# Edge pass of a graph network: gathered rows in four slots by parity of turns, attributes in another region

## The reference, cut to what matters

```python
src = edge_index[0]; dst = edge_index[1]          # 200000 edges, dst sorted
msg = jax.nn.relu(h[src] + edge_attr)             # h: [12500, 128], edge_attr: [200000, 128]
aggr = jax.ops.segment_sum(msg, dst, num_segments=n)
z = (1.0 + eps) * h + aggr                        # then two matmuls with batch norms
```

## Time and profile before

| | us |
|---|---|
| median of 3 runs | 16836.19 (16834.64 to 16855.76) |
| the profiled execution | 16957.4 |
| its span | 16955.6 |
| edge pass, first attribute load to PE's last halves (11797 to 14310) | 2513 |
| POOL busy in the whole span | 9653.8 (57%) |
| PE busy in the whole span | 6756.4 (40%) |
| DVE busy in the whole span | 3233.9 (19%) |

### The profile page before, as it was taken

The page is one execution under the profiler, slowest core; times in us unless marked ns, Lnnn a source line. Parts: engine busy times, 40 slices in busy tenths (PEclk is TensorE's granted clock), DMA queues, the critical chain, the costliest instruction groups (busy, mean ns, idle before and its releaser), DMA issues. The chain is left out here.

```text
span 16955.6 us, 119259 instructions
## 1 busy us (share of the span) xinstructions
PE 6756.4 (40%) x30243; PEld 5863.6 (35%) x30244; DVE 3233.9 (19%) x6147; ACT 824.7 (5%) x1247; POOL 9653.8 (57%) x9860
## 2 busy tenths in 40 slices
PE   3444443333334444410000009995555555533333
PEld 2333333333333333300000008873555554333333
DVE  3222221000011212200000014444111112311111
ACT  1000000000000000000000000003000000200000
POOL 2666666666666666667777440002666664366666
PEclk8555555555555555555555555557555555655555
DMA  2111111111111221233333212222222222221212
GB/s 87 47 48 47 48 48 45 48 48 48 48 47 53 55 55 54 57 87 100 100 100 99 66 33 87 97 89 84 82 81 80 82 82 89 67 54 52 54 53 53
DMA packets 593155, 1124.64 MB, mean 66 GB/s; under 512 B 220825, under 2 KB 364384, under 8 KB 566578
## 3 DMA queue, kind: packets, MB, share of 16 engines
q0 software_dynamic: 307488, 624.42, 14.6%
q1 hardware_dynamic: 285622, 499.73, 8.8%
HBM read 904.32 MB, written 218.95 MB: 66 GB/s over the span
## 5 line engine op out<-in xcount | busy, mean ns | idle before, releaser
L680 POOL DMA_INDIRECT work<-rows_a,index x4704 | 4587.5, 975 | 2399.1 <-issue 1544.6
L751 PE MATMUL psum<-onehot,work 128*128 128x64 f32 x12544 | 2822.4, 419 | 4459.8 <-DMA work<-rows_a,index 2818.1
L751 PEld LDWEIGHTS psum<-onehot,work 128*128 128x128 f32 x12544 | 2717.3, 328 | 4556.2 <-issue 4424.5
L680 POOL DMA_INDIRECT work<-rows_b,index x3136 | 3118.6, 994 | 1771.6 <-issue 1075.8
L1191 POOL DMA_INDIRECT work<-attention_rows,index x1568 | 1610.9, 1027 | 612.5 <-issue 557.2
L751 PE MATMUL psum<-onehot,regionB 128*128 128x64 f32 x6272 | 1551.9, 416 | 720.1 <-issue 581.2
L751 PEld LDWEIGHTS psum<-onehot,regionB 128*128 128x128 f32 x6272 | 1440.3, 327 | 819.6 <-issue 801.5
L846 DVE TENSOR_TENSOR regionA<-regionA,psum 128x64 f32 x2352 | 508.0, 216 | 5289.9 <-remote 2271.8
L765 PE MATMUL psum<-onehot,regionB 128*4 128x64 f32 (+1 forms) x6272 | 1174.7, 358 | 484.9 <-issue 484.5
L765 PEld LDWEIGHTS psum<-onehot,regionB 128*4 128x4 f32 (+1 forms) x6272 | 1023.8, 223 | 533.3 <-issue 486.8
L182 POOL COPY work<-regionB 128x500 f32 (+1 forms) x75 | 45.5, 606 | 2034.9 <-DVE regionB L561 2034.9
(11 more groups left out here) (253 smaller groups left out, 4471.5 us busy)
## 6 DMA issues: line engine op xcount, KB each, us to landing
gathered_rows<-work SPq DMA_DIRECT2D x98, 1088.0 KB
work<-gathered_rows SPq DMA_DIRECT2D x98, 1088.0 KB, 4.9
regionB<-in_edge_attr SPq DMA_DIRECT2D x195, 512.0 KB
work<-rows_a,index POOLq DMA_INDIRECT x4704
work<-rows_b,index POOLq DMA_INDIRECT x3136
work<-attention_rows,index POOLq DMA_INDIRECT x1568
x_transposed<-regionA SPq DMA_DIRECT2D x75, 250.0 KB, 6.0
rows_a<-regionC SPq DMA_DIRECT2D x50, 250.0 KB
```

The lines of the kernel that those rows point to most:

```text
L680: pool.indirect_dma_start(rows3[h][:, t, :], None, table, bass.IndirectOffsetOnAxis(ap=net.index[:, k, h * ST + t:h * ST + t + 1], axis=0) ...
L751: last = nc.tensor.matmul(bank_of(h, q, 0), msgs3[h][:, t, 0:D], onehot[:, h * ST + t, :], start=(k == 0), stop=(k == GT - 1))
```

## The change: what it does

In the edge pass the gathered rows get four buffers of 16 batches in region B: a pair (h = 0 and 1) for even turns and a pair for odd turns. The attributes move to `work`, and the messages lie in region B behind the four row buffers. Each row buffer has its own semaphore for landed gathers. POOL may fill a buffer when the messages that last used it are made, which is two turns earlier, not one: the counter `message[h]` starts at 2 and not at 1, and POOL's and ACT's conditions follow. At the start of a round POOL waits until all messages of the round before are made. DVE's loop over turns now runs 24 times over two turns, so that each addition knows its buffer at build time. The other passes keep their code.

```diff
-    rows3 = [r.rearrange("p (t f) -> p t f", f=width) for r in rows]
-    attr = [net.B[:, h * HALF * D:(h + 1) * HALF * D] for h in range(2)]
+    if edges:
+        rows = [[net.B[:, (k * 2 + h) * HALF * D:(k * 2 + h + 1) * HALF * D] for h in range(2)] for k in range(2)]
+    else:
+        rows3 = [r.rearrange("p (t f) -> p t f", f=width) for r in rows]
+    attr = [net.work[:, h * HALF * D:(h + 1) * HALF * D] for h in range(2)]
...
-    at0 = EPP * H if attention else 2 * HALF * D
+    at0 = EPP * H if attention else 4 * HALF * D
...
-    gathered = name("gathered") if attention else [net.pool_sem() for _ in range(S)]
+    gathered = name("gathered") if attention else [net.pool_sem() for _ in range(4 if edges else S)]
+    fills = [NIT - NIT // 2, NIT // 2]
...
-                                act.wait_ge(message[h], n + 2)
+                                act.wait_ge(message[h], n + 3)
...
+                    if edges:
+                        for h in range(2):
+                            pool.wait_ge(message[h], r * NIT + 2)
+                        pool.sem_inc(moved, 1)
...
+                            to = rows[k][h].rearrange("p (t f) -> p t f", f=D) if edges else rows3[h]
+                            landed = gathered[k * 2 + h] if edges else gathered[h]
                             for t in range(ST):
                                 pool.indirect_dma_start(
-                                    rows3[h][:, t, :], None, table,
+                                    to[:, t, :], None, table,
                                     bass.IndirectOffsetOnAxis(ap=net.index[:, k, h * ST + t:h * ST + t + 1], axis=0)
-                                ).then_inc(gathered[h], 16)
+                                ).then_inc(landed, 16)
...
-                    dve.sem_inc(message[h], 1)
+                    dve.sem_inc(message[h], 2 if edges else 1)
...
-                nc.vector.memset(net.B[:, 0:2 * HALF * D], 0.0)
+                nc.vector.memset(net.work[:, 0:2 * HALF * D], 0.0)
...
-                        dve.wait_ge(gathered[h], n * 16 * ST + 16 * ST)
+                        dve.wait_ge(gathered[k * 2 + h], (r * fills[k] + fill) * 16 * ST + 16 * ST)
                         dve.wait_ge(attr_loaded[h], n * 32 + 32)
-                        nc.vector.tensor_tensor(msgs[h], rows[h], attr[h], ALU.add).then_inc(message[h], 1)
+                        nc.vector.tensor_tensor(msgs[h], rows[k][h], attr[h], ALU.add).then_inc(message[h], 1)
...
+                if edges:
+                    with dve.Fori(0, NIT // 2) as j:
+                        for k in range(2):
+                            i = dve.snap(j * 2 + k)
+                            stage_index(net, dve.snap(i + 2), k).then_inc(index_ready, 1)
+                            for h in range(2):
+                                add(i, h)
+                                compare(dve.snap(i + 1), h)
+                                messages(dve.snap(i + 1), h, 1 - k, dve.snap(j + k))
```

More of the change, by code:

```diff
@@ L814, in compare, with messages @@
                             AX_X, ALU.add).then_inc(piled[h], 1)
-                def messages(i, h):
+                def messages(i, h, k=0, fill=0):
                     n = r * NIT + i
@@ L858, in _ @@
                     messages(0, h)
[L859 to L869, removed]
+                if edges:
[7 more added lines that the diff above has]
+                                messages(dve.snap(i + 1), h, 1 - k, dve.snap(j + k))
+                else:
+                    with dve.Fori(0, NIT - 1) as i:
+                        if not attention:
+                            following = dve.snap(i + ahead)
+                            stage_index(net, following, following % 2).then_inc(index_ready, 1)
+                        for h in range(S):
+                            add(i, h)
+                            if follow and h == S - 1:
+                                due_chunks(net, dve, i, i + 1, lambda c: follow.vector(dve, c),
+                                           lambda: all_added((r * NIT + i) * 2 * GPH + 2 * GPH))
+                            compare(dve.snap(i + 1), h)
+                            messages(dve.snap(i + 1), h)
                 for h in range(S):
```

## The result

The kernel after takes **16953.8 us** (16940.79 to 17003.71, 5 runs), the kernel before, timed again beside it, 16839.87 us (16834.64 to 16855.76, 5 runs). The ratio is 1.0084, with a 95% interval from 1.007 to 1.0097: 114 us slower. The forecast was 16860 us, no change. The time lies in the range of 16600 to 17000 us, but it is 94 us above the point, and slower was only the second likeliest direction.

What follows compares the result with a forecast made beforehand. PE, slowed beside running gathers, was taken to bound the edge pass. Terms 0 + 46 - 28 gave +18 us, +36 with the profiler's waits; +24 was taken: 16860 us, no change, range 16600 to 17000.

Steps and rivals of the forecast that it cites:

- What bounds the pass: Edge pass: PE bounds it, though not at its speed, losing 1065.7 us to "issue" and lacking work for 19.6 us.
- The signs named ahead: Edge pass near 2500 us, about 25 POOL waits of some 20 us, "issue" not smaller, slow stretches ending near pauses.
- Term (1): POOL's larger lead in the edge pass: more rows in store do not speed PE, 0 us; upper bound 433.5 us gained.
- Term (2): POOL released for whole turns: about 24.5 pauses of 20.3 us, 64 us more, 46 without the profiler; bounds -119 to +352.
- Term (3): End of the edge pass: POOL finishes further ahead, PE works off the rest without gathers at the fast pace, -28 us.
- Terms (4) to (6): Swapped regions, DVE's two-turn loop and the wait before the first gather: 0 us each; bounds 5 us for regions, +27 for loop.
- The attribute loads: Edge pass: loads could suffer from denser gathers, but the rows show 0.1 us, next to nothing.
- Rival A: POOL's pauses are pure loss and go: 16403 us, chance 0.08; with half the wait gone 16619 us, chance 0.10.
- Rival B: POOL pauses once in every turn of the edge pass, 352 us more, 17188 us; in full, chance 0.06.
- mild form: A third of Rival B, 16950 us; chance 0.26 together with Term (2) at or above its size in the profile.

Runs made afterwards that it cites:

- the second pair: The kernel before and the kernel after, both unchanged, run and profiled again in one session: 16824.15 and 16965.09 us, ratio of the kernel after 1.008.

## Why the prediction was right or wrong

**What bounds the pass.** Right for the session of the timing: PE, slowed. The signs named ahead came in: PE's "issue" did not shrink (1065.7 to 1166.4 us; within one session 979.0 to 1166.9), PE is short of work inside the pass for some 15 us only, and its slow stretches end within some 4 to 12 us of POOL's last gather. The claim held for such sessions alone, though; in the others PE has no slow pace, and POOL bounds the same pass. The forecast did not reckon with sessions that differ, so part of its being near is luck of the session.

**Term (1), the lead: 0.** Right in effect. DVE's wait for rows went from 225.0 us to none, and its wait for attributes grew instead, 243.1 to 354.0 us. PE's own waits for work did fall, from 58.6 to 15.1 us in the second pair (19.6 to 15.7 us in the first), but its "issue" grew by 188 us (101 us) over them. The forecast's bound of 19.6 us for this gain was taken from one execution and was too small for another.

**Term (2), the release by whole turns: +46 to +64 us.** The signs of the mechanism came in, and this is the term that was sized too small. POOL's waits moved from the messages to the copy of the indices, all ahead of an even half, fewer and longer. The growth of one pause was well placed: 6.8 us expected, 381.1 / 29 = 13.1 to 536.9 / 26 = 20.7 us measured, 7.5 more. The count was not. I took bursts to be "mostly four" halves, so that 32 pauses become 24.5, a quarter less. In one session they went from 29 to 26, a tenth less, with bursts of two, four and six. That gives +156 us where 64 stood, or 46 as scaled for the sum. Against the trace, from which the term was worked out, it is 28 pauses of 19.1 us where 24.5 of 20.3 us stood, 534 us where 497 stood, and +100 us. With the gathers closer together by 38 us (30 us in that pair), for which no term stood, 119 us (71 us) remain in the stretch.

**Term (3), the end: -28 us.** Wrong. More work is left behind the last gather, 112 matmuls by the windows, and PE is fast then, both as said. But a backlog at the end is time: 55 us instead of 28 (52 instead of 32 in the first pair). The step that failed counted what this work would have cost at the slow pace as saved, while PE's slow time in the pass did not fall. In its place stands +27 (+20).

The measured terms of the second pair are +156 - 38 + 27 = 145 us, those of the first +100 - 30 + 20 = +90 us, and the runs say 141 and 114. The forecast had +24. That 145 and 141 are so near is in part chance, since the two traces lie 165.5 us apart. The range of 400 us was wide enough to hold all of this, so that the time lies in it says little; the point missed because term (2), at 46 us, was under half of what came, and term (3) had the wrong sign.

**Terms (4) to (6): 0.** Right within what can be told. The addition takes 2295 ns against 2297, and in the 15.5 ms sessions every kernel with the new regions and the loop of two turns is quicker than the kernel before, by 34 to 75 us. A separate test of them where PE is slow was not made.

**The attribute loads: nothing.** Not settled. The wait for them grew by 111 us, but DVE gets to it earlier now that it never waits for rows, which alone can make it so.

**Rival A, pauses that are pure loss.** Refuted: they grew. The same holds for fewer pauses as a gain. But one argument against it, and the step from 64 to 46 us in term (2), rested on the 121.2 us between the profiled execution and the median. That gap is spread between executions. The recorded run of the kernel before in the second comparison lies 32 us below its median, and its plain passes are some 20 to 40 us shorter each than in the trace. Nothing may be derived from one such gap. Nor does the slow pace come from recording: in the 15.5 ms sessions the recorded executions have none.

**Rival B.** In full, a pause in every turn, it did not come. Its mild form, 16950 us, is where the time fell, and it had a share of 0.26 together with a larger term (2). That its number is near is luck: pauses per turn went from 29 / 49 to 26 / 49, and what grew was their length.

**What stays open.** Shown: in the 16.8 ms session the change costs 141 us, and the traces have nearly all of it as PE's slow time in the edge pass; in a 15.5 ms session it takes 35 us off. Argued only: that the release by whole turns is the cause of the loss; the kernels that would tell it from the longer lead ran in 15.5 ms sessions alone. Seen in every burst as a coincidence and never tested: that POOL's gathers make PE slow and its pauses make it fast. Not known: what makes the sessions differ, and where the 35 us come from, since the edge pass of the unchanged kernel was not recorded there.

## What to carry to other kernels

A deeper ring helps only if its reader starves because its writer is stopped. Here the writer was stopped where PE hardly lacked work, and rows were short where the writer was never stopped; in neither was there much to gain. So see first which side waits, and if the writer waits, ask what makes the reader slow. Count a release by its coarsest gate: here four buffers were released by a copy of indices that comes once a turn, and pauses became longer. Compare two traces only from one session, with the kernel before timed beside them, and do not read a mechanism out of the gap between one recorded execution and a median.

## What the runs showed of the hardware

The same program takes some 16820 us in some sessions and 15490 us in others, each within 0.5% of itself, at a granted clock of 0.50 in the pass in both. In the former, instructions of PE stand 0.7 us or more apart for long stretches beside POOL's gathers, 0.58 per us instead of 4.7, with "issue" as the only reason, and in the stretch looked at no code is loaded. In the latter, the same instructions beside the same gathers have no such gap, and also a plain pass is shorter. A window over most of one in the kernel after there:

```profile
2300.00:4330.00 2030.00, 803.93 (x3286) 716.49 (x3287) 242.91 (x574) 45.21 (x74) 1492.45 (x1541) 0.50 0.21 53
```

From its first to its last gather this pass takes 2028 us, as against 2250 us in the same kernel in the 16.8 ms session. Most of the difference is pauses of POOL: from 2610 to 4390 us it waits 191.1 us for releases there and 17.7 us here. So a change can have one sign in one session and the other in the next, here +0.8% and -0.25%, both with intervals that leave out zero.

A gather of 128 rows holds POOL for 0.94 us when no large DVE instruction runs beside it, and for up to 3 us when it starts under DVE's addition of two operands in SBUF; it then ends some 0.8 us after the addition.
